# The shared hidden tile of a Fourier MLP's second layer: three 384-column float32r products, or two 64-row float32 products in banks of their own

## The reference

```python
xf = jnp.fft.rfft2(x, axes=(1, 2), norm='ortho')          # 4, 128, 65, 8 blocks, 96
o1r = relu(xr @ w1[0] - xi @ w1[1] + b1[0])
o1i = relu(xi @ w1[0] + xr @ w1[1] + b1[1])
o2r = o1r @ w2[0] - o1i @ w2[1] + b2[0]
o2i = o1i @ w2[0] + o1r @ w2[1] + b2[1]
o = softshrink(stack([o2r, o2i]), 0.01)
out = irfft2(complex(o), s=(128, 128), axes=(1, 2), norm='ortho') + x
```

## Time and profile before

| | |
|---|---|
| median of 3 runs | 5919.63 us (5910.64 to 5933.79) |
| the profiled execution | 5931.3 us, span of its instructions 5929.5 us |
| mean granted clock of TensorE | 0.986 |
| PE busy | 5750.8 us, 97% of the span, 42048 matmuls |
| PEld busy | 5699.5 us, 96% |
| ACT busy | 3655.1 us, 62% |
| DVE busy | 3077.5 us, 52% |
| POOL busy | 1263.1 us, 21% |
| DMA | 27.8% of the 16 engines' time in the main queue |

### The profile page before, as it was taken

How to read it: one execution, slowest core, us unless ns; L and a number is a source line. 1 busy time by engine, 2 the same in 40 slices (tenths; PEclk the granted TensorE clock), 3 DMA queues, 4 the chain that set the end, 5 groups by cost and what they waited for, 6 DMA issues and landing times.

```text
span 5929.5 us, 116828 instructions
## 1 busy us (share of the span) xinstructions
PE 5750.8 (97%) x42048; PEld 5699.5 (96%) x42048; DVE 3077.5 (52%) x6166; ACT 3655.1 (62%) x8208; POOL 1263.1 (21%) x810
## 2 busy tenths in 40 slices
PE   8999999999999999999999999999999999999997
PEld 8999999999999999999999999999999999999997
DVE  4555545555455554555545555455554455544555
ACT  6656666566665666656566565665656656566564
POOL 2211222202222022220222202222022221122200
PEclk9999999999999999999999999999999999999999
DMA  3331133321333113332133321333312333123311
GB/s 94 89 89 40 50 89 89 89 50 41 89 89 89 46 44 89 89 89 59 33 88 89 89 68 31 80 89 89 79 34 66 89 89 87 39 53 89 89 44 43
DMA packets 1109645, 423.36 MB, mean 71 GB/s; under 512 B 1108768, under 2 KB 1108896, under 8 KB 1109024
## 3 DMA queue, kind: packets, MB, share of 16 engines
q1 hardware_dynamic: 1109024, 415.14, 27.8%
HBM read 213.75 MB, written 201.33 MB: 70 GB/s over the span
## 4 chain that ended last, share of the span: by engine, by line
PE 96%; issue 2%; ACT 1%; DVE 1%; DMA 0%; DVEq 0%; SPq 0%; ACTq 0%
PE psum L499 16%; PE psum L523 12%; PE psum L512 12%; PE psum L558 12%; PE psum L513 12%; PE psum L542 6%; PE psum L544 6%; PE psum L538 3%; PE psum L570 3%; PE psum L541 3%; PE psum L540 3%; PE psum L539 3%; PE psum L571 3%; PE psum L572 3%; DVE x L465 1%
## 5 line engine op out<-in xcount | busy, mean ns | idle before, releaser
L440 DVE TENSOR_SCALAR relu<-psum,b1t 128x128 f32<-128x128 f32 x1056 | 370.3, 351 | 1936.2 <-ACT hidden_high L355 1936.1
L289 POOL TENSOR_TENSOR doubled<-x 128x768 f32<-128x768 f32 x248 | 359.0, 1447 | 4337.2 <-DMA x<-x 4317.0
L512 PE MATMUL psum<-w1t,columns 96*128 96x192 f32 x4160 | 1035.8, 331 | 66.7 <-ACT columns L313 66.7
L513 PE MATMUL psum<-w1t,columns 96*128 96x192 f32 x4160 | 1029.7, 329 | 0.0
L499 PEld LDWEIGHTS psum<-mats,x 128*96 128x96 f32 x8192 | 930.0, 168 | 76.4 <-issue 54.2
L499 PE MATMUL psum<-mats,x 128*96 128x128 f32 x8192 | 939.1, 278 | 65.5 <-issue 48.8
L349 ACT ACTIVATE mixed<-psum 128x384 f32<-128x384 f32 (+1 forms) x1056 | 513.6, 486 | 746.7 <-PE psum L513 741.6
L376 ACT ACTIVATE sums_high<-psum 128x512 fp32r<-128x512 f32 x768 | 460.0, 599 | 763.7 <-PE psum L558 763.7
L523 PE MATMUL psum<-mats,mixed 128*128 128x128 f32 x6272 | 877.3, 276 | 0.0
L523 PEld LDWEIGHTS psum<-mats,mixed 128*128 128x128 f32 x6272 | 845.5, 193 | 0.0
L512 PEld LDWEIGHTS psum<-w1t,columns 96*128 96x128 f32 x4160 | 756.1, 199 | 73.5 <-ACT columns L313 73.5
(11 more groups left out here) (61 smaller groups left out, 8437.8 us busy)
## 6 DMA issues: line engine op xcount, KB each, us to landing
x<-x SPq DMA_DIRECT2D x160, 768.0 KB, 7.2
out<-x SPq DMA_DIRECT2D x160, 768.0 KB, 8.2
x<-x SPq DMA_DIRECT2D x32, 1488.0 KB, 9.7
out<-x SPq DMA_DIRECT2D x32, 1488.0 KB, 10.6
x<-x SPq DMA_DIRECT2D x32, 816.0 KB, 5.0
out<-x SPq DMA_DIRECT2D x32, 816.0 KB, 4.5
w2t<-L_conv_w SPq DMA_DIRECT2D x128, 36.0 KB
w2t<-L_conv_w SPq DMA_DIRECT2D x128, 24.0 KB
```

The lines of the kernel that those rows point to most:

```text
L512: pe.matmul(bank_b(s)[:, k], re, w1t[par][:, BLOCK:], start=True, stop=False)
L513: last = pe.matmul(bank_b(s)[:, k], im, w1t[par][:, :2 * BLOCK], start=False, stop=True)
```

## The change

In the second layer the middle tile is no longer split. DVE writes its ReLU once, in float32 (`middle`), straight after `c_done`. PE multiplies it as two float32 matmuls of 64 rows: partitions 0 to 63 with the first column's weights into the first column's sums, and 64 to 127 with the second's. The sums of the two columns now lie in two banks (4 and 5, or 6 and 7 by parity), 96 values at a time with a stride of 256, and the bias is two matmuls of 192 columns. For these banks `stage_c` gives up its second set: it always uses banks 2 and 3, and waits for the ReLUs of the step just before. `flip`, which uses bank 6, waits for `shrunk` of step 31 in place of step 0. `hidden_high`, `hidden_low`, `relu1`, `w2_high`, `w2_low` and the four DVE operations per unit that filled the last two are gone.

```diff
         def bank_c(s):
 
-            outer = bank(2 + s % 2, SIZE, 2 * SIZE)
-            return [outer[:, 0:SIZE], bank(6 + s % 2, SIZE, SIZE), outer[:, SIZE:]]
+            outer = bank(2, SIZE, 2 * SIZE)
+            return [outer[:, 0:SIZE], bank(3, SIZE, SIZE), outer[:, SIZE:]]
 
         def bank_d(s):
-            return bank(4 + s % 2, SIZE, 4 * BLOCK)
+
+            pair = psum[:, 4 + 2 * (s % 2):6 + 2 * (s % 2), :].rearrange("p k n -> p (k n)")
+            return pair.rearrange("p (q n) -> p q n", q=4)[:, :, 0:BLOCK]
...
                             act.wait_ge(c_done, n * NS + (t + 1))
-                            act.activation(hidden_high[t % 2][:, :], bank_c(t)[1], ACT.Relu,
-                                           bias=b1t[par][:, 1:2]).then_inc(high_done, 1)
...
-                            dve.wait_ge(high_done, n * NS + (s + 1))
-                            dve.tensor_scalar(relu1[s % 2][:, :], bank_c(s)[1], b1t[par][:, 1:2], 0.0,
-                                              ALU.add, ALU.max).then_inc(relu1_done, 1)
-                            dve.wait_ge(relu1_done, n * NS + (s + 1))
-                            dve.tensor_tensor(hidden_low[s % 2][:, :], relu1[s % 2][:, :], hidden_high[s % 2][:, :],
-                                              ALU.subtract).then_inc(low_done, 1)
+                            dve.wait_ge(c_done, n * NS + (s + 1))
+                            dve.tensor_scalar(middle[s % 2][:, :], bank_c(s)[1], b1t[par][:, 1:2], 0.0,
+                                              ALU.add, ALU.max).then_inc(middle_done, 1)
...
             def stage_c(n, s):
                 pe.wait_ge(b_copied, n * NS + (s + 1))
-                if s >= 2:
-                    pe.wait_ge(relu_done, n * NS + (s - 1))
-                    pe.wait_ge(relu1_done, n * NS + (s - 1))
+                if s >= 1:
+                    pe.wait_ge(relu_done, n * NS + s)
+                    pe.wait_ge(middle_done, n * NS + s)
...
                 pe.wait_ge(relu_done, n * NS + (s + 1))
-                pe.wait_ge(low_done, n * NS + (s + 1))
+                pe.wait_ge(middle_done, n * NS + (s + 1))
                 if s >= 2:
                     pe.wait_ge(shrunk, n * NS + (s - 1))
-                one, both = 2 * BLOCK, len(STEPS[s]) * 2 * BLOCK
-                h, high, low, w, sums_d = hidden[s % 2], hidden_high[s % 2], hidden_low[s % 2], w2t[par], bank_d(s)
-                bias = b2_parts[:, :].unsqueeze(1).broadcast_to([SIZE, len(STEPS[s]), 2 * BLOCK])
-                pe.matmul(sums_d[:, 0:both].rearrange("p (k o) -> p k o", o=2 * BLOCK), picks[:, :], bias, start=True, stop=False)
-                pe.matmul(sums_d[:, 0:both], high[:, :], w2_high[:, 0:both], start=False, stop=False)
-                pe.matmul(sums_d[:, 0:both], low[:, :], w2_high[:, 0:both], start=False, stop=False)
-                pe.matmul(sums_d[:, 0:both], high[:, :], w2_low[:, 0:both], start=False, stop=False)
-                last = pe.matmul(sums_d[:, 0:one], h[:, 0], w[:, 0:one], start=False, stop=both == one)
-                if both > one:
-                    last = pe.matmul(sums_d[:, one:both], h[:, 1], w[:, 2 * one:], start=False, stop=True)
+                h, mid, w, kws = hidden[s % 2], middle[s % 2], w2t[par], range(len(STEPS[s]))
+                sums_d = [bank_d(s)[:, 2 * k:2 * k + 2] for k in kws]
+                outer = [w[:, 0:2 * BLOCK], w[:, 4 * BLOCK:]]
+                for k in kws:
+                    pe.matmul(sums_d[k], picks[:, :], b2_parts[:, :].rearrange("p (r c) -> p r c", r=2), start=True, stop=False)
+                for k in kws:
+                    pe.matmul(sums_d[k], h[:, k], outer[k].rearrange("p (r c) -> p r c", r=2), start=False, stop=False)
+                for k in kws:
+
+                    half = slice(k * HALF, (k + 1) * HALF)
+                    last = pe.matmul(sums_d[k], mid[half, :], w[half, 2 * BLOCK:4 * BLOCK].rearrange("p (r c) -> p r c", r=2),
+                                     start=False, stop=True)
                 last.then_inc(d_done, 1)
 
             def flip(n):
-                pe.wait_ge(shrunk, n * NS + 1)
+                pe.wait_ge(shrunk, n * NS + (NS - 1))
```

More of the change, by code:

```diff
@@ L109, in fourier_mlp @@
         hidden = [sb(f"hidden{i}", [SIZE, 2, SIZE]) for i in range(2)]
-        hidden_high, hidden_low = ([sb(f"hidden_{x}{i}", [SIZE, SIZE], F32R) for i in range(2)] for x in ("high", "low"))
-        relu1 = [sb(f"relu1_{i}", [SIZE, SIZE]) for i in range(2)]
+        middle = [sb(f"middle{i}", [SIZE, SIZE]) for i in range(2)]
         excess = [sb(f"excess{i}", [SIZE, BLOCK, 4]) for i in range(2)]
@@ L123, in fourier_mlp @@
         w2t = [sb(f"w2t{i}", [SIZE, 6 * BLOCK]) for i in range(2)]
-        w2_high, w2_low = (sb(f"w2_{x}", [SIZE, 4 * BLOCK], F32R) for x in ("high", "low"))
         over = sb("over", [SIZE, 1])
@@ L155, in bank_c @@
         def bank_c(s):
-            outer = bank(2 + s % 2, SIZE, 2 * SIZE)
-            return [outer[:, 0:SIZE], bank(6 + s % 2, SIZE, SIZE), outer[:, SIZE:]]
+            outer = bank(2, SIZE, 2 * SIZE)
+            return [outer[:, 0:SIZE], bank(3, SIZE, SIZE), outer[:, SIZE:]]
         def bank_d(s):
-            return bank(4 + s % 2, SIZE, 4 * BLOCK)
+            pair = psum[:, 4 + 2 * (s % 2):6 + 2 * (s % 2), :].rearrange("p k n -> p (k n)")
+            return pair.rearrange("p (q n) -> p q n", q=4)[:, :, 0:BLOCK]
         def parts_d(s, rows):
-            return bank_d(s).rearrange("p (q c) -> p c q", c=BLOCK)[:, :, 0:rows]
+            return bank_d(s).rearrange("p q c -> p c q")[:, :, 0:rows]
         bank_flip = bank(6, SIZE, 2 * BLOCK).rearrange("p (k c) -> p k c", k=2)
@@ L185, in fourier_mlp @@
         padding_set = sem("padding_set")
-        w_negated, w2_split = sem("w_negated"), sem("w2_split")
-        high_done, relu1_done, low_done = sem("high_done"), sem("relu1_done"), sem("low_done")
+        w_negated = sem("w_negated")
+        middle_done = sem("middle_done")
         u_zeroed = sem("u_zeroed")
@@ L379, in _ @@
         def _(dve):
-            for t in (w2_high, w2_low):
-                dve.memset(t[HALF:SIZE, 0:2 * BLOCK].bitcast(F32), 0.0).then_inc(padding_set, 1)
-                dve.memset(t[0:HALF, 2 * BLOCK:].bitcast(F32), 0.0).then_inc(padding_set, 1)
             dve.memset(over[:, :], -LAMBDA).then_inc(padding_set, 1)
@@ L385, in _ @@
             dve.memset(picks[:, :].bitcast(F32), 0.0).then_inc(padding_set, 1)
-            dve.wait_ge(padding_set, 7)
+            dve.wait_ge(padding_set, 3)
             for row in (0, LOW_ROW):
@@ L420, in _ @@
                         dve.tensor_scalar(part, part, -1.0, None, ALU.mult).then_inc(w_negated, 1)
[L422 to L425, removed]
                     dve.tensor_copy(b2_parts[0:1, :], b2t[par][0:1, :]).then_inc(b2_split, 1)
@@ L575, in _ @@
             pe.wait_ge(mats_loaded, 16)
-            pe.wait_ge(padding_set, 9)
+            pe.wait_ge(padding_set, 5)
             with pe.Fori(0, PAIRS) as m:
```

1 line of the change is left out of this document (removed).

## The result

The changed kernel takes 6174.34 us (median of 4, 6171.56 to 6177.83) against 5918.97 of the kernel before in the same comparison: ratio 1.0428, 95% interval 1.041 to 1.0447, so +255 us. Slower was forecast, but at 5972 us and 0.9%; the change cost almost five times that. 6174 lies inside the range of 5925 to 6240, between the two prices of the emptying rival (6141 and 6310).

A forecast was written before the change was run, and what follows sets the result against it. PE's slots were taken to bound the steps. +41 us for the steps, -2 for the dropped `hidden_low` wait and +13 for the flip made +52, giving 5972 us (+0.9%) on the median; range 5925 to 6240.

The forecast's parts named there:

- emptying rival: Array must empty at both row changes of a step: up to 2 x 0.16 us, 6310; half price 6141; chance 0.20.
- The bound, and what gets nothing: In the steps only PE's slots count; work taken from ACT or DVE there pays nothing.
- The bias: In each step's second layer, two float32r matmuls of 192 columns at the pace of their loads: 0.22 us.
- the single set of `stage_c` banks: `stage_c` waits for the ReLUs of the step before, covered by `stage_d` and `stage_b`: cost 0.
- the flip: At each unit's end, waiting for step 31's shrink starts it 0.41 us later: +13 us over 32 units.
- Changing between 64-row and 128-row matmuls ... I take 0: Around each step's halves: a change costs 0 to 0.16 us each time; taken as 0, like 96 to 128 rows.
- Only the middle two can overlap: Of the middle tile's four 64-row records, only the second and third share time: 0.53 us a step.
- side by side throughout: Rival: each half runs high and low independently on its own rows, 0.33 us in place of 0.53: 5762; chance 0.13.
- at one of the two places: Cheaper case of emptying: the array empties only going into the halves or only coming out: 6141.
- The order of the records: Middle tile's records start in program order: first half high, first half low, second half high, second half low.

The follow-up runs named there:

- e6: The kernel before with `stage_c` always on banks 2 and 3, waiting for the ReLUs of the step just before: ratio 1.0005.
- e5: The kernel before with only the flip's wait changed, to the shrink of step 31 in place of step 0: ratio 1.0013.
- e7: The changed kernel with both 64-row matmuls of each step issued twice, one pair behind the other: 6510.7 us, ratio 1.0949 to the kernel before.
- e3: The kernel before with only its bias matmul taking partitions 0 to 63 in place of all 128: 6318.2 us, ratio 1.0644.
- e2: The changed kernel without the second half's matmul: 6172.8 us, ratio 1.0393 to the kernel before.

## Why the prediction was wrong

The bound, and what gets nothing: right. The chain within a step is PE's alone before and after, and 860 us less work on DVE and ACT gave nothing.

The bias (0.22 forecast, 0.21 measured), the single set of `stage_c` banks (0 in the changed kernel, where the forecast's 0.3 us less of `hidden_high` pays for the one place that e6 shows to wait) and the flip (+13 forecast, 0.41 us a unit in e5's trace) stand.

The step that failed is "Changing between 64-row and 128-row matmuls ... I take 0". It measured 0.41 us a step, 0.21 in and 0.20 out (e7, and the L497 pieces). That is above even the bound given there, 2 x 0.16. The reason for taking 0, that 96 and 128 rows follow each other free of charge, was a row of the wrong kind: the 96-row matmuls of `stage_b` follow and precede 128 rows freely, and L497 pays in full behind a block of 64. In these runs the price is paid between 64 rows and 96 or 128, and the trace of before had no case of it. The bound was too low since it held only the emptying, for which 0.08 to 0.09 is left. A load that doesn't go ahead of the change adds its 0.11 each time; the loads' pace of the earlier trace rows would have given it. The Trainium skill (TensorEngine Tiling (Array Packing), Key Properties) states that a change of tiling mode drains TensorE. The runs fit that, with a remainder of 0.08 us for it in e3, and show 0.11 us of uncovered load on top.

The second error hid behind a sum that was right by luck. "Only the middle two can overlap", and so 0.53 us for the halves: the piece is 0.53, but it is 0.32 of work and 0.21 of way in. The halves go side by side (e2: the second half costs 0.01). The rival "side by side throughout" was right about the work, and wrong about the time, since it came with the changes. "The array must empty" was right about the cause, but it was priced on top of a step in which the halves mostly took turns. Neither rival alone gives 6174. Together they do: 0.21 + 0.02 + 0.32 + 0.41 - 0.71 = +0.25 a step, x 1024 = 256, and the flip's 13 on top make 269. The units' own stretches at the upper level show 262 (8.09 + 0.09 us for each of 32), and of these the clock gave some back, so that the medians differ by 255. The rival's price for emptying "at one of the two places" (6141) comes near for the same luck: the way in was already in the 0.53. That 6174 lies in the range is luck in part: the case in it that has the changes puts them at half of 0.16 and on top of a step that was wrong.

The order of the records failed as well. "First half high, first half low, second half high, second half low" is not how they start. The traces don't show whether they are issued in these pairs, or whether TensorE reorders them, so this doesn't decide if "in all rows matmuls start in the order of the program" fails for matmuls on separate rows.

## What to carry to other kernels

Two matmuls on separate halves of the rows, each with its own bank, cost as much as one. But stepping from 128 rows to 64 and back to 96 or 128 costs some 0.4 us here, more than two of the float32r matmuls of 384 columns (0.18 each), so a block of 64-row work must be long enough to pay for it: one pair lost 4%, a block of two steps with the bias in it won 1%, 0.6% of it in the steps themselves. A matmul that takes 64 rows only because the rest is zero is not free to do so amid full ones (e3: 6%); let it take all 128. And a busy share of 97% can hide gaps of 0.2 us: compare the chain's pieces of one and the same line.

## What the runs showed of the hardware that was not expected

- Float32 matmuls of two halves, written as first half then second, start in two pairs, one record of each half in each: two within 0.03 us, and four in flight later. Their weight loads go in pairs too (x4 in 0.30 us; the two loads of one float32r bias pair of 128 rows take the same 0.30).
- At a change between 64 rows and 96 or 128 no weight load goes ahead (on both sides of the halves the load engine sits idle for 0.23 us). Elsewhere in the step a load starts with the matmul ahead of it. The uncovered load is 0.11 of each 0.20.
- One bias matmul of 64 rows in place of 128 in each step made the kernel before 6.4% slower, though all that it leaves out is a multiplication by zeros (e3).
